# Second attention of a PixArt-style stack: the first mixture's sums and post-norm one batch further ahead, and their addition to x on GpSimd

## The reference

```python
x = x + attention0(layernorm(x), ctx)
x = x + mixture0(layernorm(x))          # 8 experts, the best 2 of each row; ends in its own layernorm
x = x + attention1(layernorm(x), ctx)
x = x + quantum_ffn(layernorm(x))
x = x + window_attention(ctx, layernorm(x))
x = x + mixture2(layernorm(x))          # 8 experts, the best 2 of each row; no layernorm at its end
x = x + attention3(layernorm(x), ctx)
x = x + ternary_ffn(layernorm(x))
```

```python
u = z + w0 * y0 + w1 * y1
x = x + ((u - mean(u)) * rsqrt(var(u) + 1e-5) * g + b)    # g, b: L0_ffn_ln_g, L0_ffn_ln_b
```

## Time and profile before

| | |
|---|---|
| runs | 2239.66, 2240.86, 2243.93 us; median 2240.86 |
| profiled execution | 2244.04 us, its span 2242.2 us |
| TensorE busy | 1940.1 us (87%) |
| VectorE busy | 1318.4 us (59%) |
| ScalarE busy | 935.3 us (42%) |
| GpSimd busy | 596.2 us (27%) |
| mean granted TensorE clock | 0.933 of full |

### The profile page before, as it was taken

The page is one execution under the profiler, slowest core; times in us unless marked ns, Lnnn a source line. Parts: engine busy times, 40 slices in busy tenths (PEclk is TensorE's granted clock), DMA queues, the critical chain, the costliest instruction groups (busy, mean ns, idle before and its releaser), DMA issues. The chain is left out here.

```text
span 2242.2 us, 37690 instructions
## 1 busy us (share of the span) xinstructions
PE 1940.1 (87%) x11915; PEld 1447.4 (65%) x11931; DVE 1318.4 (59%) x3008; ACT 935.3 (42%) x2057; POOL 596.2 (27%) x598
## 2 busy tenths in 40 slices
PE   6999469999848897999979659999999987997687
PEld 3677346666525564566667459999999974664455
DVE  5877656666558886787645542222222216887887
ACT  2544124444346543333224223333333323553787
POOL 1122346666424431011000132222222221321000
PEclk9999579999969998999989669999999997999899
DMA  7000211111141104000001511111111114100001
GB/s 275 11 20 30 78 57 63 61 61 63 51 165 57 57 1 165 0 0 0 0 22 46 197 38 38 36 35 37 37 35 35 37 32 157 39 20 1 10 29 38
DMA packets 71267, 119.68 MB, mean 53 GB/s; under 512 B 13664, under 2 KB 54880, under 8 KB 68096
## 3 DMA queue, kind: packets, MB, share of 16 engines
q1 hardware_dynamic: 55904, 78.89, 10.1%
q0 software_dynamic: 13680, 37.37, 5.2%
q10 hardware_dynamic: 1584, 2.13, 0.3%
HBM read 87.03 MB, written 31.33 MB: 53 GB/s over the span
## 5 line engine op out<-in xcount | busy, mean ns | idle before, releaser
L1440 ACT ACTIVATE e_hT<-psum,x_bt 128x128 f32<-128x128 f32 x568 | 154.6, 384 | 336.4 <-PE psum L1403 331.8
L269 POOL TENSOR_TENSOR rstd<-lnt,half 128x4 f32<-128x4 f32 (+1 forms) x72 | 73.3, 1018 | 778.0 <-DVE lnt L263 778.0
L1403 PEld LDWEIGHTS psum<-e_xT,e_w 128*128 128x128 f32 x2272 | 268.3, 194 | 8.4 <-ACT e_xT L1433 4.9
L1403 PE MATMUL psum<-e_xT,e_w 128*128 128x128 f32 x2272 | 268.9, 277 | 4.2 <-ACT e_xT L1433 4.2
L1412 PE MATMUL psum<-m_w,e_hT 128*128 x1136 | 256.8, 379 | 0.0
L1461 DVE COPY e_w<-m_w 128x2048 f32 x71 | 87.1, 1227 | 238.3 <-PE psum L1403 233.9
L1412 PEld LDWEIGHTS psum<-m_w,e_hT 128*128 128x128 f32 x1136 | 210.4, 190 | 25.7
L758 DVE TENSOR_REDUCE a_mx<-psum 128x8 f32<-128x512 f32 x192 | 123.2, 684 | 80.8 <-PE psum L533 80.3
L1260 ACT ACTIVATE e_hT<-psum,x_bt,x_gt 128x128 f32<-128x128 f32 x284 | 106.9, 457 | 145.0 <-PE psum L1227 145.0
L1344 POOL DMA_INDIRECT rows_out<-e_y,dst x106 | 106.0, 1000 | 208.6 <-DVE e_y L1471 175.0
L1336 POOL DMA_INDIRECT e_x<-rows_in,src x142 | 142.1, 1001 | 56.4 <-issue 35.4
(11 more groups left out here) (298 smaller groups left out, 3559.1 us busy)
## 6 DMA issues: line engine op xcount, KB each, us to landing
m_w<-in_L_ffn_w SPq DMA_DIRECT2D x16, 1024.0 KB, 12.0
m_w<-in_L_ffn_w SPq DMA_DIRECT2D x16, 512.0 KB, 11.9
m_w<-rows_out SPq DMA_DIRECT2D x16, 512.0 KB, 5.9
a_ar_g<-rows_out SPq DMA_DIRECT2D x16, 512.0 KB, 5.1
rows_in<-a_r_z SPq DMA_DIRECT2D x14, 512.0 KB, 2.9
x_res<-in_x SPq DMA_DIRECT2D x8, 512.0 KB, 7.1
m_w<-rows_in SPq DMA_DIRECT2D x8, 512.0 KB, 3.9
out_x<-x_res SPq DMA_DIRECT2D x8, 512.0 KB, 3.0
```

Source lines behind the costliest of these rows:

```text
L1403: mm = pe.matmul(h_b[s][:, f, :], w1[:, kk, f * P:(f + 1) * P], xT[s][:, kk, :], start=(kk == 0), stop=(kk == DC - 1))
L1440: g = act.activation(hT[s][:, f, :], h_b[s][:, f, :], ACT.Gelu, bias=bt[:, bass.ds(e * FC + f, 1)])
```

## The change

In attention 1, three buffers (`R = 3`) take the place of two for `u` and the two `y`, so that `fetch(b)` waits for the batch three back. The sum and its norm run one batch further ahead:

- VectorE: `sum_statistics(b + 3)` at t = 1 (was b + 2 at t = 0); `add_sum` is gone from its step.
- GpSimd: the order in a step is gain(b + 2), add_sum(b + 2), u_norm.root(b + 3), add_bias(b + 1), in_norm.root(b + 2), out_norm.root(b - 2), sum(b + 4).
- ScalarE: `normalise_sum(b + 3)` at t = 3, right behind `normalise(b + 2)` (was b + 2 at t = 1); `scale` of batch b + 4 in four pieces of two tiles instead of two of four.
- Before the first step: sum(3), sum_statistics(2), u_norm.root(2), the scales of batch 3 and normalise_sum(2) are done ahead.

In attentions 1 and 3 the outgoing norm's moments of batch b - 2 stand at t = 1 (were b - 1 at t = 2), and those of batch 6 stand behind the last scaling, ahead of the last three residuals. Attention 0 keeps its order.

```diff
+        lag = 1 if router else 2
...
                 pool.wait_ge(k.att_in, 16 * k.att_loads)
                 add_bias(0)
+                if normed:
+                    normed.u_norm.root(pool, 2)
+                    normed.sum(pool, 3)
                 for b in range(NB):
...
                     if normed:
                         if b + 2 < NB:
-                            normed.u_norm.root(pool, b + 2)
+                            normed.gain(pool, b + 2)
+                            normed.add_sum(pool, b + 2)
+                        if b + 3 < NB:
+                            normed.u_norm.root(pool, b + 3)
                         if b + 1 < NB:
                             add_bias(b + 1)
-                        if b + 2 < NB:
-                            normed.gain(pool, b + 2)
-                        if b + 3 < NB:
-                            normed.sum(pool, b + 3)
                     if in_norm and b + 2 < NB:
                         in_norm.root(pool, b + 2)
-                    if b > 0:
-                        out_norm.root(pool, b - 1)
+                    if b >= lag:
+                        out_norm.root(pool, b - lag)
+                    if normed and b + 4 < NB:
+                        normed.sum(pool, b + 4)
...
-                        if normed and b + 2 < NB and t == 1:
-                            normed.normalise_sum(act, b + 2)
-                        if normed and b + 3 < NB and t in (0, 2):
-                            normed.scale(act, t // 2, b + 3)
+                        if normed and b + 4 < NB and t < 2:
+                            normed.scale(act, 0, b + 4, (2 * t, 2 * t + 1))
+                        if normed and b + 4 < NB and t in (1, 2):
+                            normed.scale(act, 1, b + 4, (2 * t - 2, 2 * t - 1))
                         if t == 3 and b + 2 < NB:
                             normalise(b + 2)
+                        if normed and t == 3 and b + 3 < NB:
+                            normed.normalise_sum(act, b + 3)
...
                         normed.scale(act, j, 2)
                     normalise(1)
+                    for j in range(TOPK):
+                        normed.scale(act, j, 3)
+                    normed.normalise_sum(act, 2)
...
-                        if normed and t == 0 and b + 2 < NB:
-                            normed.sum_statistics(dve, b + 2)
-                        if normed and t == 2 and b + 2 < NB:
-                            normed.add_sum(dve, b + 2)
+                        if normed and t == 1 and b + 3 < NB:
+                            normed.sum_statistics(dve, b + 3)
...
-                        if t == 2 and b > 0:
-                            out_norm.moments(dve, b - 1)
+                        if t == 3 - lag and b >= lag:
+                            out_norm.moments(dve, b - lag)
...
                 drain_keys(1, 1)
+                if normed:
+                    normed.sum_statistics(dve, 2)
                 for b in range(NB):
                     step(b, b % 2)
                 scale(2 * NB - 1, 1)
+                if lag > 1:
+                    out_norm.moments(dve, NB - 2)
...
+R = 3
...
-        self.u = [part(r) for r in range(2)]
-        self.y = [[part(2 + 2 * j + r) for r in range(2)] for j in range(TOPK)]
+        self.u = [part(r) for r in range(R)]
+        self.y = [[part(R + R * j + r) for r in range(R)] for j in range(TOPK)]
...
-        wait_pos(sp, self.x_done, b - 1)
+        wait_pos(sp, self.x_done, b - R + 1)
```

More of the change, by code:

```diff
@@ L481, in _ @@
                             router.add_post(pool, b - 3)
-                out_norm.root(pool, NB - 1)
+                for b in range(NB - lag, NB):
+                    out_norm.root(pool, b)
                 if router:
@@ L1567, in __init__ @@
         part = lambda i: k.w2[:, i * (TPB * D):(i + 1) * (TPB * D)].rearrange("p (t d) -> p t d", t=TPB)
-        self.u = [part(r) for r in range(2)]
-        self.y = [[part(2 + 2 * j + r) for r in range(2)] for j in range(TOPK)]
+        self.u = [part(r) for r in range(R)]
+        self.y = [[part(R + R * j + r) for r in range(R)] for j in range(TOPK)]
         self.g = sb(nm + "g", [P, D])
         self.u_shift = sb(nm + "u_shift", [P, NT])
-        self.rows_in = [sem(f"{nm}rows_in{r}") for r in range(2)]
+        self.rows_in = [sem(f"{nm}rows_in{r}") for r in range(R)]
         self.g_in, self.scaled, self.part, self.summed, self.u_done, self.u_scaled, self.x_done = (
@@ L1600, in sum_alone, with scale @@
                     dve.wait_ge(self.part, n + 1)
-                dve.scalar_tensor_tensor(at, self.y[j][b % 2][:, t, :], self.k.wt[j][:, n:n + 1], at,
+                dve.scalar_tensor_tensor(at, self.y[j][b % R][:, t, :], self.k.wt[j][:, n:n + 1], at,
                                          ALU.mult, ALU.add).then_inc(done, 1)
-    def scale(self, act, j, b):
+    def scale(self, act, j, b, tiles=range(TPB)):
         self.landed(act, b)
-        for t in range(TPB):
-            n, at = b * TPB + t, self.y[j][b % 2][:, t, :]
+        for t in tiles:
+            n, at = b * TPB + t, self.y[j][b % R][:, t, :]
             o = act.activation(at, at, ACT.Copy, scale=self.k.wt[j][:, n:n + 1])
-        o.then_inc(self.scaled, 1)
+        if t == TPB - 1:
+            o.then_inc(self.scaled, 1)
     def sum(self, pool, b):
-        u = self.u[b % 2]
+        u = self.u[b % R]
         for j, done in enumerate((self.part, self.summed)):
@@ L1624, in sum_statistics @@
             dve.wait_ge(self.summed, b * TPB + t + 1)
-            self.u_norm.statistics(dve, b * TPB + t, self.u[b % 2][:, t, :])
+            self.u_norm.statistics(dve, b * TPB + t, self.u[b % R][:, t, :])
         self.u_norm.moments(dve, b)
```

18 lines of the change are left out of this document (9 added, 9 removed).

## The result

| | before | changed |
|---|---|---|
| median of 20 runs each, us | 2242.43 | 2239.39 |
| lowest to highest | 2239.50 to 2247.03 | 2234.74 to 2242.45 |
| profiled execution, us (its span) | 2244.04 (2242.2) | 2241.93 (2240.1) |

The ratio is 0.9985, with a 95% interval of [0.9978, 0.9992]: 3.4 us faster, between 1.8 and 4.9. I had forecast 8.8. A later comparison of the same two kernels gave 0.998 [0.9969, 0.9992].

A forecast was written before the change was run, and what follows sets the result against it. Attention 1's batches of 28.05 us had VectorE busy for 24.2, with TensorE's floor near 22. Start, batches, attention 3 and the two ends summed to -8.8 us, median 2240.86 to 2232.1, range 2225.5 to 2239.5.

The forecast's parts named there:

- start (batch 0): Attention 1's first batch: the sum's normalisation in front of the first exponents costs +4.2 us, bounds +1.5 and +7.4.
- batch 1: Attention 1: without GpSimd's conflict, the batch goes from 28.04 to 24.9 us, -3.1.
- batches 2 to 4: Attention 1: with outgoing moments waiting for GpSimd's bias, each goes from 28.05 to 26.0 us, -6.15 together.
- batch 5: Attention 1: still with the sum's normalisation in front, it goes from 25.41 to 24.9 us, -0.5.
- batch 6: Attention 1: without the sum's normalisation in front, it takes 22.85 us against 23.36, -0.5.
- attention 3 to its last batch: Outgoing moments move into a gap before the fourth softmax: five batches gain 0.77 us, the last full one 0.5, -4.35.
- the conflict with the bias: Attention 1, batches 2 to 4: GpSimd's bias addition holds VectorE's last outgoing moments, making batches 26.0 us; cost 1.1 each.
- Rival 1: Outgoing moments slip through before GpSimd's bias: batches 2 to 4 take 24.9, -12.2 us in all, 2228.7; chance 0.18.
- Rival 3: GpSimd's roots hold VectorE too, delaying outgoing moments: +0.35 us in three batches, +1.0, 2233.1; chance 0.06.
- Rival 5: Slower than before: TensorE's clock stays at 1.2 GHz through batch 0, +8.6 us in all, 2249.5; chance 0.05.
- rival 2: TensorE half-clock stretches before z's second transposes cost 1.7 us each in batches 1 and 5: +3.4, 2235.5; chance 0.14.
- Rival 4: The start costs its upper bound, +7.4 us, and half-clock stretches add 3.4: -2.2 in all, 2238.7; chance 0.11.

The follow-up runs named there:

- bias_late: The changed kernel with GpSimd's root of the outgoing statistics ahead of the bias addition; 2233.56 us, ratio 0.9967 to the kernel before.
- warm2: The changed kernel with 8 more matmuls in batch 0 of attention 1, ahead of the second batch's first transposes; 2237.80 us, ratio 0.9978 to before.
- lag_only: The kernel before with only the outgoing moments moved, one tile earlier and two batches behind, and their GpSimd root likewise; 2231.27 us, ratio 0.9966.
- sums_only: The changed kernel with the outgoing moments back at their old place, one batch behind; 2239.03 us, ratio 0.9995 to the kernel before.
- swap: The changed kernel with ScalarE normalising the sum before z instead of after it; 2226.97 us, ratio 0.9957 to the kernel before.
- reorder: swap plus outgoing moments before VectorE's first scaling, the last ones before the last scaling, and GpSimd's list spread out; 2221.46 us, ratio 0.9922 to before.
- start_fix2: start_fix with the fifth batch's sum on GpSimd put behind the root of the incoming statistics in batch 0; 2218.53 us, ratio 0.9901 to before.
- start_fix: reorder with the old start: third batch's sum normalised after the second tile's exponents, fourth sum made within batch 0; 2218.86 us, ratio 0.9890 to before.
- moments_t0: The changed kernel with attention 1's outgoing moments moved in front of VectorE's first scaling; 2243.77 us, ratio 0.9998 to the kernel before.

## Why the forecast was right in mechanism and wrong in size

Each term of the sum, with what two profiled executions of the changed kernel show against the first one of the kernel before (us):

| term | forecast | first | second |
|---|---|---|---|
| start (batch 0) | +4.2 | +5.6 | +5.1 |
| batch 1 | -3.1 | -3.2 | -1.5 |
| batches 2 to 4 | -6.15 | -5.4 | -5.3 |
| batch 5 | -0.5 | +1.1 | -0.6 |
| batch 6 | -0.5 | -0.5 | -0.5 |
| last batch of attention 1 | 0 | +0.5 | +0.5 |
| end of attention 1 | +0.8 | +1.3 | +1.7 |
| attention 3 to its last batch | -4.35 | -4.4 | -4.4 |
| last batch of attention 3 | 0 | +0.5 | +0.5 |
| end of attention 3 | +0.8 | +1.0 | +0.8 |
| sum | -8.8 | -3.5 | -3.7 |

The sums of the two last columns stand within the interval of the ratio, 1.8 to 4.9 (the end of attention 1 is read from the last softmax to the feed-forward's first f_zT on ScalarE, 23.30 before, 24.62 and 24.99 after; that of attention 3 to the end of its last projection, 12.51 before, 13.57 and 13.30 after). They leave out the stretch between the attentions, of which below.

- *The mechanisms held.* The batch of 24.9 with ScalarE's extra 2.0 us, the conflict with the bias at 1.1, the batch of 22.85, attention 3 at 23.25, the first exponents at 670.5: each came within 0.15 of its row. Rival 1, moments that slip through, did not happen, though the margin was 0.01 to 0.11 us and not 0.2: that the side of it was right is partly luck. By `bias_late` it would have been worth its 1.1 in a batch without a stretch and next to nothing in one with: batches 2 to 4 are together 1.0 shorter there, not 3.4. Rival 3 fell with the 0.15 us row inside GpSimd's root. Rival 5 did not happen: TensorE's 0.86 in batch 0 cost 1.4, not 17.4.
- *The step that failed* is the clock in the sum. I put the half-clock stretches at nothing in the forecast's sum and made them rival 2, with a chance of 0.14 and a price of 1.7 in batches 1 and 5 alone. Both profiled executions of the changed kernel had them. I read the earlier trace rows rightly, that a stretch costs nothing in a batch of 28.05, but that was true because VectorE was the bound there. I had made TensorE's path the bound by my own sum, so each stretch had to appear in it. Three of the five batches had one, at 1.7 in batch 1 or 5. I also let the bias hide it wholly; it left 0.5 to 0.6 in batches 2 to 4. Over batches 1 to 5 that is 2.2 and 2.4 us. The start adds 1.4 and 0.9, the last projection of attention 1, 1.67 and 2.04 instead of 1.10, another 0.6 and 0.9. Together some 4.2 of the missing 5.2 (mean of the two columns).
- *The other 1.0* is batch 6. Its moments went away from before the next softmax, 0.5 in each attention, but the next scores came no sooner: TensorE's scores of the last batch's first two tiles are 4.94 apart in both kernels (837.65 and 842.59 before, 836.00 and 840.94 after). The first tile of the last batch took 4.94 instead of 4.42, and the 0.5 was gone.
- *The start's order* was right at +4.2: `warm2` measures 23.75 - 19.61 = 4.1. Rival 4 took 7.4 for it and was wrong, though its total, 2238.7, came near the measured one through the stretches of rival 2 that it included.
- *What I didn't see* could be read without any run: the change did several things at once, and I never priced the moments alone. By the earlier trace rows, the place at t == 1 had 2.41 us idle and the old one 1.25 of blocking and 0.77 of work, and these were nearly all of a batch's gain. `lag_only` is faster than the change: its attention 1 is 7.6 us shorter.

What stays open: between attention 1 and attention 3 nothing was edited, yet from the last softmax of the one to the first of the other the profiled executions differ by up to 7 us (1020.39 in `sums_only`, 1027.66 in the first of the changed kernel, 1023.19 in its second). In one kernel it is 4.5. What decides that isn't shown. It also stays open why the ratios of `lag_only`, `swap`, `reorder` and `start_fix2` give 3 to 5 us less than their two attentions with their ends do (10.8, 14.6, 22.6 and 26.2 us shorter in the profiled executions).

## What to carry to other kernels

When a change removes the bound of a stage, price the disturbances that the old bound covered: here half-clock stretches that cost 0 in a batch bound by VectorE cost 1.7 us each once TensorE's chain was the bound. Price each part of a combined change by itself, as one part may carry the gain and another give it back. And for every small VectorE instruction ask which wide GpSimd instruction runs beside it, and set the lists of both engines so that they don't meet; an order set on three engines took attention 1 from 191.81 to 175.79, where ScalarE's order alone gave 180.62 and the move of the moments to t = 0 alone 195.08.

## What I had not expected of the hardware

- GpSimd's additions over 128x1024 held VectorE's instructions over 128x4 until their end: with two inputs (L255, 1.61; L257, 2.32), with a scalar and two inputs (L259, 2.32 in `start_fix`), and with one input and a number (L260, 2.33 in `moments_t0`). The addition to x in the earlier trace rows, 2.62 us long beside L1619, takes 1.22 where no such instruction runs (639.16). One over 128x256 did it too: in attention 3 of the changed kernel L318 starts at 1936.03, and L263 at 1936.18 takes 0.61.
- Beside the same GpSimd instructions VectorE's statistics (L245, 1.40 for four) and all that reads PSUM (softmax, scaling, residual) kept their times in both attentions of every kernel here. GpSimd's root over 128x4 held none: 36 additions and subtractions of the moments started inside one in the two attentions of the fourteen profiled executions, each at its usual time. In the batch of 29.38, one small instruction slipped in between two wide ones.
- TensorE's stretches at 1.2 GHz landed in other batches from one execution of the changed kernel to the next, while the total of attention 1 repeated within 0.4 us; in the kernel before they stayed in batches 1, 3 and 5. Filling the hole of 4.14 us in front of one of them brought the first batch's clock from 0.86 to 1.00, and the later batches had four stretches instead of three.
- `reorder`, with no idle time of TensorE over 0.58 us in batches 1 to 6, has no stretch there: its granted clock is 1.00, where the changed kernel's is 0.94 in three. That the gap of 2.07 us brings the stretch about is likely by where they begin and by `swap`: without that gap batches 1 and 5 had none, and its one stretch, in batch 4 (0.93), lies behind another gap of 1.99. But no run changed a gap and nothing else.
